# Half-width steps share PSUM banks four deep, the half job goes through f16, two weight pieces are split before the first SiLU

## What is computed

```python
def layer0(h, gates, shared, Wg, Wu, Wd, Sg, Su, Sd):
    g = einsum('bsd,edf->ebsf', h, Wg)
    u = einsum('bsd,edf->ebsf', h, Wu)
    experts = einsum('ebsf,efd->ebsd', silu(g) * u, Wd)
    expert = einsum('be,ebsd->bsd', gates, experts)
    both = einsum('bsf,fd->bsd', silu(h @ Sg) * (h @ Su), Sd)
    return (1 - shared) * expert + shared * both

def layer1(h, lang, W1, b1, W2, b2, gamma, beta):
    a = relu(h @ W1[lang] + b1[lang])
    y = h + a @ W2[lang] + b2[lang]
    return layernorm(y) * gamma[lang] + beta[lang]

x = x + layer0(x, ...)
x = x + layer1(x, ...)
```

## Time and profile before

| what | value |
|---|---|
| median of 3 runs | 296.86 us |
| lowest, highest | 296.78 us, 297.94 us |
| the profiled execution | 297.13 us |
| its span, first to last instruction | 295.3 us |
| PE busy | 290.9 us (99% of the span) |
| DVE busy | 267.9 us (91%) |
| ACT busy | 231.0 us (78%) |
| mean granted TensorE clock | 0.996 |

### The profile page before, as it was taken

How to read it: one execution, slowest core, us unless ns; L and a number is a source line. 1 busy time by engine, 2 the same in 40 slices (tenths; PEclk the granted TensorE clock), 3 DMA queues, 4 the chain that set the end, 5 groups by cost and what they waited for, 6 DMA issues and landing times.

```text
span 295.3 us, 5098 instructions
## 1 busy us (share of the span) xinstructions
PE 290.9 (99%) x1515; PEld 145.7 (49%) x1515; DVE 267.9 (91%) x584; ACT 231.0 (78%) x515; POOL 18.8 (6%) x32
## 2 busy tenths in 40 slices
PE   8999999999999999999999999999999999999995
PEld 4444444444444444444444444444444444588883
DVE  4999999998989898988989999999999999977795
ACT  6998878788878787877897788887878876667771
POOL 3200201100000000000001010001100011000011
PEclk9999999999999999999999999999999999999998
DMA  7973110244000000000011001010001110000001
GB/s 205 373 322 109 51 66 20 60 119 114 3 2 0 2 0 0 0 2 1 1 23 25 18 9 39 12 25 21 18 0 39 26 19 10 2 36 3 0 2 36
DMA packets 17940, 13.39 MB, mean 45 GB/s; under 512 B 11486, under 2 KB 15994, under 8 KB 17914
## 3 DMA queue, kind: packets, MB, share of 16 engines
q1 hardware_dynamic: 17482, 12.86, 14.5%
q10 hardware_dynamic: 432, 0.21, 0.2%
HBM read 11.23 MB, written 1.05 MB: 42 GB/s over the span
## 4 chain that ended last, share of the span: by engine, by line
PE 98%; DVE 1%; POOL 0%; POOLq 0%; issue 0%; DVEq 0%
PE up_ps L445 11%; PE gate_ps L396 10%; PE moe_ps L468 10%; PE moe_ps L471 10%; PE up_ps L437 10%; PE moe_ps L469 10%; PE up_ps L440 10%; PE gate_ps L397 10%; PE gate_ps L402 10%; PE moe_ps L512 1%; PE adapt_ps L480 0%; DVE w_lo L689 0%; PE gate_ps L411 0%; PE moe_ps L452 0%; PE x_ps L497 0%; PE gate_ps L414 0%
## 5 line engine op out<-in xcount | busy, mean ns | idle before, releaser
L588 ACT ACTIVATE silu<-gate_ps 128x512 f32<-128x512 f32 (+1 forms) x160 | 88.5, 553 | 46.1 <-PE gate_ps L402 44.4
L705 DVE SCALAR_TENSOR_TENSOR hidden<-silu,up_ps 128x512 f32<-128x512 f32 (+1 forms) x160 | 101.2, 633 | 19.7 <-PE up_ps L445 12.0
L711 DVE TENSOR_TENSOR h_lo<-hidden,h_hi 128x512 f16<-128x512 f32 (+1 forms) x159 | 103.8, 653 | 0.2
L593 ACT ACTIVATE h_hi<-hidden 128x512 f16<-128x512 f32 (+1 forms) x159 | 92.4, 581 | 8.9 <-DVE hidden L705 8.1
L445 PE MATMUL up_ps<-gx_hi,w_lo 128*128 128x512 f16 (+1 forms) x160 | 57.2, 358 | 0.1
L437 PE MATMUL up_ps<-gx_hi,w_hi 128*128 128x512 f16 (+1 forms) x160 | 57.3, 358 | 0.0
L440 PE MATMUL up_ps<-gx_lo,w_hi 128*128 128x512 f16 (+1 forms) x160 | 57.2, 358 | 0.0
L469 PE MATMUL moe_ps<-h_hi,w_lo 128*128 128x512 f16 (+1 forms) x159 | 56.9, 358 | 0.0
L468 PE MATMUL moe_ps<-h_hi,w_hi 128*128 128x512 f16 (+1 forms) x159 | 56.9, 358 | 0.0
L471 PE MATMUL moe_ps<-h_lo,w_hi 128*128 128x512 f16 (+1 forms) x159 | 56.9, 358 | 0.0
L396 PE MATMUL gate_ps<-x_hi,w_hi 128*128 128x512 f16 (+1 forms) x158 | 56.5, 358 | 0.0
(11 more groups left out here) (95 smaller groups left out, 154.7 us busy)
## 6 DMA issues: line engine op xcount, KB each, us to landing
w_full<-weights SPq DMA_DIRECT2D x8, 768.0 KB, 9.0
affine_sb<-affine SPq DMA_DIRECT2D x16, 128.0 KB, 2.9
x_full<-xT SPq DMA_DIRECT2D x3, 256.0 KB, 8.4
x<-x_blocks SPq DMA_DIRECT2D x48, 16.0 KB, 1.8
out_dram<-result SPq DMA_DIRECT2D x3, 256.0 KB, 2.0
w_full<-weights SPq DMA_DIRECT2D x4, 128.0 KB, 3.2
w_full<-w2b SPq DMA_DIRECT2D x24, 16.0 KB
w_full<-weights SPq DMA_DIRECT2D x1, 256.0 KB, 3.9
```

Source lines behind the costliest of these rows:

```text
L588: nc.scalar.activation(silu_slot(n), gate_ps[n % 2][:, 0:STEPS[n][4]], ACT.Silu, scale=1.0 / W_SCALE).then_inc(silu_ready, 1)
L593: nc.scalar.activation(h_slot(h_hi, n), hidden_slot(n), ACT.Copy).then_inc(h_hi_ready, 1)
L705: nc.vector.scalar_tensor_tensor(out=hidden_slot(n), in0=silu_slot(n), scalar=HIDDEN_RESCALE * (W_SCALE if n < WHOLE_STEPS else 1), in1=up ...
L711: nc.vector.tensor_tensor(h_slot(h_lo, n), hidden_slot(n), h_slot(h_hi, n), ALU.subtract).then_inc(h_lo_ready, 1)
```

## The change

It has four parts.

- **Banks.** From the first half step on, gate and up of a step lie in the two halves of one bank, and the four gate and up banks go round: step n uses bank n mod 4 of them (`half_ps`). `silu_of(n)` of a half step waits for `up(n)` and not for `gate(n)`. `gate(n)` waits for the hidden of step n - 4, and `up(n)` for nothing of the kind. `silu` is cut into four slots.
- **Lag.** `END_LAG` is 7, so step 154 has no `down` either, and seven `down`s stand behind the last step.
- **Job 3.** It goes the way of jobs 0 to 2, at a width of 256 columns. `w2_upper` on ACT is 8 steps ahead of `at` and `w2_lower` on DVE 6 steps ahead. `adapter_relu` writes `h_full`; `h_upper` on ACT and two instructions of `h_others` on DVE build the stack at step 151; `adapter_back` is two f16 matmuls behind step 154 (it was step 153); y is one DVE instruction of 256 columns, and what follows it is one step later. Loads of two sequences bring w2 in four pieces and not one.
- **Front.** The hi parts of pieces 2 and 3 both stand ahead of `silu_of(0)` on ACT, and their lo parts ahead of `hidden_of(0)` on DVE.

```diff
-END_LAG = 6
+END_LAG = 7
+FIRST_HALF = len(WHOLE)
...
 def back_at(j):
-    return 6
+    return 6 if j < MOVED else 7
+def w2_at(j):
+    return 0 if j < MOVED else -8
...
+        odd = FIRST_HALF % 2
+        half_ps = [gate_ps[odd], up_ps[odd], gate_ps[1 - odd], up_ps[1 - odd]]
+        def gate_at(n):
+            return gate_ps[n % 2][:, :] if n < FIRST_HALF else half_ps[(n - FIRST_HALF) % 4][:, 0:HALF]
+        def up_at(n):
+            return up_ps[n % 2][:, :] if n < FIRST_HALF else half_ps[(n - FIRST_HALF) % 4][:, HALF:N]
         def silu_slot(n):
-            return silu[:, n % 2 * N:n % 2 * N + STEPS[n][4]]
+            return cols(silu, n % 2, N) if n < FIRST_HALF else cols(silu, n % 4, HALF)
...
-                    if t == last_tile:
+                    if t == last_tile and q >= TAIL[1]:
...
-                pe.wait_ge(silu_ready, n - 1)
+                if n < FIRST_HALF:
+                    pe.wait_ge(silu_ready, n - 1)
+                elif n < FIRST_HALF + 2:
+                    pe.wait_ge(hidden_ready, FIRST_HALF - 1)
+                elif n == FIRST_HALF + 2:
+                    pe.wait_ge(silu_ready, FIRST_HALF)
+                else:
+                    pe.wait_ge(hidden_ready, max(n - 3, FIRST_HALF))
...
-                if n > 1:
+                if 1 < n < FIRST_HALF:
                     pe.wait_ge(hidden_ready, n - 1)
...
             def adapter_back(j):
...
-                pe.wait_ge(adapt_h_ready, count)
-                pe.wait_ge(x2_ready, 1)
+                pe.wait_ge(w2_lower_ready, j + 1)
+                pe.wait_ge(h_others_ready, 2 * (j + 1))
+                if j >= MOVED:
+                    pe.wait_ge(x2_ready, 1)
                 for q in range(first, first + count):
-                    last = nc.tensor.matmul(cols(back_ps[q % 2], q // 2, D), stacked(adapt_h, q, S, A + 1),
-                                            stacked(w2b2_sb, q, D, A + 1), start=True, stop=True)
+                    last = nc.tensor.matmul(cols(x2_ps, q, D), cols(h_stack, q, S, STACK), cols(w2_stack, q, D, STACK),
+                                            start=True, stop=True)
...
             def silu_of(n):
-                act.wait_ge(gate_done, n + 1)
-                if n > 1:
+                if n < FIRST_HALF:
+                    act.wait_ge(gate_done, n + 1)
+                else:
+                    act.wait_ge(up_done, n + 1)
+                if n >= FIRST_HALF:
+                    act.wait_ge(hidden_ready, max(n - 3, FIRST_HALF))
+                elif n > 1:
                     act.wait_ge(hidden_ready, n - 1)
...
                 if n == 0:
                     first_weight_hi(2)
+                    first_weight_hi(3)
                 silu_of(n)
-                if n == 0:
-                    first_weight_hi(3)
...
-                    if n == at and j < MOVED:
+                    if n == at + w2_at(j):
                         w2_upper(j)
...
-                    if n == at + in_at(j) + 2 and j < MOVED:
+                    if n == at + in_at(j) + 2:
                         h_upper(j)
...
-                    if j < MOVED:
-                        nc.vector.scalar_tensor_tensor(out=y[:, :], in0=x2_ps[:, :], scalar=OUT_RESCALE, in1=x2[:, :],
-                                                       op0=ALU.mult, op1=ALU.add).then_inc(y_ready, BATCHES)
-                if j >= MOVED:
-                    nc.vector.tensor_tensor(cols(y, q, D), cols(back_ps[q % 2], q // 2, D), cols(x2, q, D),
-                                            ALU.add).then_inc(y_ready, 1)
+                    width = JOBS[j][2] * D
+                    nc.vector.scalar_tensor_tensor(out=y[:, 0:width], in0=x2_ps[:, 0:width], scalar=OUT_RESCALE,
+                                                   in1=x2[:, 0:width], op0=ALU.mult,
+                                                   op1=ALU.add).then_inc(y_ready, JOBS[j][2])
...
-                if since == 2 and j < MOVED:
+                if since == w2_at(j) + 2:
                     w2_lower(j)
-                if since == 4 and j < MOVED:
+                if since == in_at(j) + (3 if j < MOVED else 2):
                     h_others(j)
...
                 if n == 0:
                     first_weight_lo(2)
+                    first_weight_lo(3)
                 hidden_of(n)
...
-                if n == 0:
-                    first_weight_lo(3)
```

More of the change, by code:

```diff
@@ L276, in adapter_count @@
         def adapter_count(t):
-            return 16 * BATCHES * (6 * (t + 1) if t < last_tile else 6 * t + 3)
+            return 16 * (6 * BATCHES * (t + 1) if t < last_tile else 6 * (B - TAIL[2]) + 3 * TAIL[2])
         def fourth(tensor, q):
@@ L388, in gate @@
                 t, e, f, at, width = STEPS[n]
[L389 removed]
+                hi, lo, psum = expert_w(w_hi, e, 0, f), expert_w(w_lo, e, 0, f), gate_at(n)
                 x_at = slice(t * N + at, t * N + at + width)
@@ L544, in _ @@
                 if i == 0:
-                    pe.wait_ge(adapt_h_ready, JOBS[-1][2] + 1)
+                    pe.wait_ge(adapt_h_ready, 1)
                 else:
@@ L584, in silu_of @@
             def silu_of(n):
-                act.wait_ge(gate_done, n + 1)
-                if n > 1:
+                if n < FIRST_HALF:
[5 more added lines that the diff above has]
+                elif n > 1:
                     act.wait_ge(hidden_ready, n - 1)
-                nc.scalar.activation(silu_slot(n), gate_ps[n % 2][:, 0:STEPS[n][4]], ACT.Silu,
+                nc.scalar.activation(silu_slot(n), gate_at(n), ACT.Silu,
                                      scale=1.0 / W_SCALE).then_inc(silu_ready, 1)
@@ L599, in adapter_relu @@
                 for q in range(first, first + count):
[L600 to L605, removed]
+                    nc.scalar.activation(cols(h_full, q, S, A), fourth(adapt_ps, q)[:, 0:S], ACT.Relu,
+                                         bias=fourth(b1_sb, q)[:, 0:1]).then_inc(h_full_ready, 1)
             def w2_upper(j):
@@ L610, in w2_upper @@
                     act.wait_ge(back_done, j)
-                nc.scalar.activation(w2_stack[:, :], w2_full[:, :], ACT.Copy, scale=W_SCALE).then_inc(w2_upper_ready, 1)
+                width = JOBS[j][2] * D
+                nc.scalar.activation(w2_stack[:, 0:width], w2_full[:, 0:width], ACT.Copy,
+                                     scale=W_SCALE).then_inc(w2_upper_ready, 1)
             def h_upper(j):
                 act.wait_ge(h_full_ready, BEFORE[j + 1])
-                nc.scalar.activation(h_stack[0:A, :], h_full[:, :], ACT.Copy, scale=H_SCALE).then_inc(h_upper_ready, 1)
+                width = JOBS[j][2] * S
+                nc.scalar.activation(h_stack[0:A, 0:width], h_full[:, 0:width], ACT.Copy,
+                                     scale=H_SCALE).then_inc(h_upper_ready, 1)
             def copy_x2(j):
@@ L730, in w2_lower @@
                 dve.wait_ge(w2_upper_ready, j + 1)
-                nc.vector.scalar_tensor_tensor(out=w2_stack[2 * A:STACK - 1, :], in0=w2_full[2 * A:STACK - 1, :], scalar=W_SCALE,
-                                               in1=w2_stack[2 * A:STACK - 1, :], op0=ALU.mult,
+                width = JOBS[j][2] * D
+                nc.vector.scalar_tensor_tensor(out=w2_stack[2 * A:STACK - 1, 0:width], in0=w2_full[2 * A:STACK - 1, 0:width],
+                                               scalar=W_SCALE, in1=w2_stack[2 * A:STACK - 1, 0:width], op0=ALU.mult,
                                                op1=ALU.subtract).then_inc(w2_lower_ready, 1)
@@ L736, in h_others @@
                 dve.wait_ge(h_upper_ready, j + 1)
-                nc.vector.tensor_scalar(h_stack[2 * A:3 * A, :], h_full[:, :], H_SCALE, None, ALU.mult).then_inc(h_others_ready, 1)
-                nc.vector.scalar_tensor_tensor(out=h_stack[A:2 * A, :], in0=h_full[:, :], scalar=H_SCALE, in1=h_stack[0:A, :],
-                                               op0=ALU.mult, op1=ALU.subtract).then_inc(h_others_ready, 1)
+                width = JOBS[j][2] * S
+                nc.vector.tensor_scalar(h_stack[2 * A:3 * A, 0:width], h_full[:, 0:width], H_SCALE, None,
+                                        ALU.mult).then_inc(h_others_ready, 1)
+                nc.vector.scalar_tensor_tensor(out=h_stack[A:2 * A, 0:width], in0=h_full[:, 0:width], scalar=H_SCALE,
+                                               in1=h_stack[0:A, 0:width], op0=ALU.mult,
+                                               op1=ALU.subtract).then_inc(h_others_ready, 1)
             def norm_stats(j, i):
```

14 lines of the change are left out of this document (3 added, 11 removed).

## The result

The changed kernel takes **297.54 us** (median, 297.31 to 297.92), the kernel before 296.75 in the same measurement: ratio 1.0024, 95% interval 1.0018 to 1.0029. That is slower by 0.2%, inside the 0.5% that the prediction called "within", and 0.5 us above its 297.0. The profiled execution took 297.31, with a span of 295.5.

The account below looks back on a forecast made before the run. PE was taken as the bound (busy 290.9 of 295.3 us), with DVE deciding the end. 297.13 - 0.22 (front) + 0.39 (job) = 297.30 for the profiled execution, 0.27 above the median: 297.0 us, range 296.0 to 298.0.

Parts of the forecast that it names:

- The half steps: Steps of half width: SiLU waits for up, 0.33 later, hidden by h_lo's cover of 1.12; no change in time.
- The job on ACT and DVE: Job 3 from step 150 to the last down: DVE falls behind PE, last matmul at 289.45 against 289.06, plus 0.39.
- the second from 281.19 to 281.61 (0.42 for 256 columns): Second part of job 3's h_others on DVE: takes 0.42, after which hidden(152) starts at 281.64.
- this kind of collision in the front: POOL's cast could block piece 3's lo part on DVE; up(2) then waits 0.1 and the front brings 0.12.
- PE's stall: Behind step 154's up, adapter_back is due at 281.31 but waits for h_others until some 281.66: 0.35.
- The front: Step 2: splitting piece 3 earlier removes the hole before the third matmul of up(2), minus 0.22.
- I take the full hole, since the margin is over a microsecond: Step 2: lo part of piece 3 ends at 7.33, up(2) wants it at 8.80, so all 0.22 is gained.
- the bound of 0: Lower limit of the gain at step 2: the earlier split of piece 3 brings nothing, against minus 0.22 at most.
- The second rival: Start of the kernel: brings only 0 to 0.12, through the cast or a late piece; 297.1 to 297.3, 8%.
- The first rival: Last down: PE keeps the lead over DVE, the end gains 0.18 to 0.53; 296.5 to 296.1, 27%.

Follow-up runs that it names:

- the three edits: Changed kernel with job 3's adapter_back one step later, POOL's residual-and-beta addition held until h_lo(155), both scaled and result instructions behind the last h_lo: 296.59 us, ratio 0.9993.
- POOL was held: Changed kernel with POOL's residual-and-beta addition of job 3 waiting until both parts of h_others are done: 297.50 us, ratio 1.0026.

## Why the prediction was right, and where its size was off

The forecast (slower on the job, nothing in the half steps, within 0.5%) came true by its own mechanism. Its time was 0.5 low, for two terms. The range of 296.0 to 298.0 is wide beside a change of 0.8, so that the time fell into it says little; the rows below say more.

- **The half steps: right.** SiLU 0.33 later, no hole at the pitch of 0.109, idle times unchanged, and 267.64 for the long stretch against 267.71.
- **The job on ACT and DVE: right but for one term.** This execution reached the job 0.50 sooner than the one of the kernel before (276.24 against 276.74), so 0.50 comes off each forecast:

| | forecast - 0.50 | measured |
|---|---|---|
| SiLU(150) | 277.71 | 277.72 |
| relus | 278.30 | 278.30 |
| SiLU(151) | 279.05 | 279.05 |
| h_upper ends | 280.18 | 280.19 |
| first part of h_others | 280.36 | 280.37 |
| second part | 280.69 | 280.68 |
| second part ends | 281.11 | 281.52 |
| hidden(152) | 281.14 | 281.55 |
| hidden(154) | 282.48 | 282.89 |
| hidden(159) | 287.58 | 287.89 |
| last matmul of the last down | 288.95 | 289.27 |

ACT's rows, in answer to the earlier trace rows:

```profile
278.30 0.73 ACT L622 ACTIVATE h_full<-adapt_ps,b_sb 32x128 f32<-32x128 f32 x2
279.05 0.38 ACT L610 ACTIVATE silu<-up_ps 128x256 f32<-128x256 f32 x1
...
279.79 0.40 ACT L636 ACTIVATE h_stack<-h_full 32x256 f16<-32x256 f32 x1
```

The step that failed is "the second from 281.19 to 281.61 (0.42 for 256 columns)": it measured 0.84. The length was right for DVE alone, but the prediction did not look at POOL there, though it had weighed just this kind of collision in the front. DVE gave back 0.1 of it on the way, and the end came at +0.71 in place of +0.39. 0.32 of the miss is this.
- **PE's stall: 1.0 in place of 0.35**, of which 0.41 is the same collision. The rest is the distance from the end of the second part to the matmul: 0.26 (281.78 - 281.52), where the prediction took 0.05. It did not move the end, which DVE set.
- **The front: 0.22 taken in full, none seen.** The failed step is "I take the full hole, since the margin is over a microsecond". The margin was there for the lo part. But the hole stood in two of five traces of the old front and not in every execution, and the hi part ahead of SiLU(0) waits for a piece that landed as late as 6.65 with the new front, where the prediction had 6.35 at the latest. So the bound of 0 was the better one for the sum. The second rival (the front brings little, with "a piece that lands late") had half of this.
- **The first rival** (PE keeps the lead) is what the kernel comes near to without the new waits: the three edits bring 11.99 where it had 12.32 less 0.18 to 0.53, so 11.79 to 12.14. DVE still sets the last matmul there.

0.32 and 0.22 make 0.54; the median is 0.51 above the forecast. Taken as a change, the forecast was 297.03 - 296.86 = 0.17 and the measurement 297.54 - 296.75 = 0.79, so the miss is 0.62, of which 0.54 is named and 0.08 is within the interval.

## What to carry to other kernels

When a chain on DVE is to set the end, write beside each of its instructions with two SBUF inputs what POOL runs at that time, and where the change moves both, ask again: here a single 0.7 us addition on POOL, harmless beside a hidden, cost 0.4 beside another instruction. To get it out of the way, don't delay it by one instruction, but place it where DVE reads PSUM or a single SBUF tensor. And a hole at the start of a kernel that hangs on the landing of a transfer is to be read from more than one execution before a gain is booked for it.

## What the runs showed of the hardware

**When the blocked instruction ends.** Where a POOL instruction was running, DVE's instruction of 0.42 ended some 0.28 behind the end that the trace gives for POOL's: w_lo at 8.97 against 8.69 before, the second part at 281.52 against 281.24, h_lo(151) at 282.50 against 282.22 where POOL was held, and h_lo at 281.41 against 281.13 in the kernel before. The h_lo of 512 columns, 0.68 by itself, ended 0.55 behind (162.14 against 161.59). So DVE goes on some 0.14 ahead of POOL's recorded end, and the loss is what is left of POOL's instruction by then. Not every POOL instruction blocks for its recorded length: beside `rstd`, of two columns, from 286.81 to 287.53 in the changed kernel, an h_lo that started at 287.20 took its plain 0.42. A cast on POOL, with one input, blocks as well; in the changed kernel with the old front, DVE and POOL:

```profile
7.88 0.83 DVE L711 SCALAR_TENSOR_TENSOR w_lo<-w_full,w_hi 128x256 f16<-128x256 f32 x1
...
7.82 0.61 POOL L908 CAST x_hi<-x_full 128x512 f16<-128x512 f32 x1 [3.37 <-DMA x_full<-xT]
```

It ended at 8.71, 0.28 behind the cast's 8.43. In all of these POOL had started first. The other order is in the kernel before with the banks and the lag alone, DVE and POOL:

```profile
7.62 0.42 DVE L711 SCALAR_TENSOR_TENSOR w_lo<-w_full,w_hi 128x256 f16<-128x256 f32 x1
...
7.67 0.84 POOL L906 CAST x_hi<-x_full 128x512 f16<-128x512 f32 x1 [3.39 <-DMA x_full<-xT]
```

Here DVE started first and kept its 0.42, and the cast took 0.84 in place of 0.61. Whichever starts first goes through.

**The first matmuls run at two paces.** In the kernel before the first two gate matmuls of 256 columns took 0.61 together, in the changed one 0.39 (timeline of PE, before, then after):

```profile
4.25 0.61 PE L411 MATMUL gate_ps<-x_hi,w_hi 128*128 128x256 f16 x2
```

```profile
4.26 0.39 PE L434 MATMUL gate_ps<-x_hi,w_hi 128*128 128x256 f16 x2
```

Both paces turn up with the old front and with the new. It moves the start of everything behind it by a few tenths, which is why the stretches above begin behind it. The slow pairs start some 0.43 apart, the later ones 0.22, and the granted clock reads 1.00 from 4 to 6 us in both traces. What decides between the paces stays open.
